# Causal attention in one transformer block: one score matmul and one row-maximum unit side by side, smaller PSUM buffers, the whole stage written out, an even plan of the maxima

## The reference

```python
def attn(x, W_Q, W_K, W_V, W_o):               # x: (1, 4096, 256), 16 heads of 16
    Q, K, V = (heads(W_Q), heads(W_K), heads(W_V))
    scores = jnp.einsum('bhqd,bhkd->bhqk', Q, K) / D_HEAD ** 0.5
    scores = scores + causal                   # -inf above the diagonal
    probs = jax.nn.softmax(scores, axis=-1)
    out = jnp.einsum('bhqk,bhkd->bhqd', probs, V)
    return out.transpose(0, 2, 1, 3).reshape(B, S, D_MODEL) @ W_o

x = L0_attn_x
xn = _layernorm(x, axis=-1)
x = x + attn(xn, ...) + moe(xn, ...)           # moe: 16 experts, each takes its 512 best tokens
```

## Time and profile before

| | us |
|---|---|
| median of three runs | 2787.35 (2768.93 to 2787.67) |
| the profiled execution | 2760.16 |
| its span, first to last instruction | 2758.4 |
| its attention blocks, 194.9 to 1947.7 | 1752.8 |

### The profile page before, as it was taken

One profiled execution on the slowest core, in us unless ns is written; L12 is line 12 of the kernel. 1 busy time (PEld: TensorE's weight loads), 2 busy tenths in 40 slices (PEclk: granted clock), 3 DMA queues, 4 the chain that ended last, 5 costly groups with the idle time before them and its releaser, 6 DMA issues. The chain is left out here.

```text
span 2758.4 us, 49577 instructions
## 1 busy us (share of the span) xinstructions
PE 2553.8 (93%) x16188; PEld 1434.8 (52%) x16190; DVE 1985.1 (72%) x3851; ACT 1432.8 (52%) x1899; POOL 237.6 (9%) x210
## 2 busy tenths in 40 slices
PE   7699999999999999999999999999799599999997
PEld 4454443334433334433333443333588488888886
DVE  6588788866888876788887788893455366666664
ACT  3205555665555565555666555568332244444543
POOL 0120000000000000000000000000110123333333
PEclk9859899998999998899999999999899799999999
DMA  7730000011000012000002100000121344444444
GB/s 254 271 110 25 9 9 9 1 57 52 11 9 9 9 38 58 22 11 9 9 9 59 44 9 3 3 3 3 56 68 53 124 115 123 123 123 123 123 123 123
DMA packets 141711, 165.12 MB, mean 60 GB/s; under 512 B 38848, under 2 KB 104896, under 8 KB 141504
## 3 DMA queue, kind: packets, MB, share of 16 engines
q1 hardware_dynamic: 128832, 144.08, 16.1%
q0 software_dynamic: 12672, 18.42, 3.9%
HBM read 115.50 MB, written 46.43 MB: 59 GB/s over the span
## 5 line engine op out<-in xcount | busy, mean ns | idle before, releaser
L794 DVE TENSOR_REDUCE a_mp<-a_pm 128x1 f32<-128x512 f32 (+3 forms) x2304 | 1332.1, 638 | 273.7 <-PE a_pm L873 169.7
L850 ACT ACTIVATE a_p<-a_ps 128x1024 f32<-128x1024 f32 (+3 forms) x1152 | 1039.9, 952 | 747.3 <-PE a_ps L914 513.5
L873 PE MATMUL a_pm<-a_k,a_q 48*128 48x512 f32 (+3 forms) x2304 | 874.6, 490 | 83.0 <-DVE a_mp L794 47.5
L873 PEld LDWEIGHTS a_pm<-a_k,a_q 48*128 48x128 f32 x2304 | 377.3, 195 | 757.6 <-DVE a_mp L794 689.1
L914 PE MATMUL a_ps<-a_q,a_k 50*128 50x512 f32 (+3 forms) x2304 | 662.4, 445 | 21.8 <-ACT a_p L850 13.1
L930 PE MATMUL a_po<-a_p,a_v 128*32 128x512 f32 (+3 forms) x4608 | 604.7, 599 | 0.1
L914 PEld LDWEIGHTS a_ps<-a_q,a_k 50*128 50x128 f32 x2304 | 288.2, 193 | 112.0 <-ACT a_p L850 83.6
L1321 DVE TENSOR_TENSOR e_hf<-e_g,e_pu 128x512 f32<-128x512 f32 x128 | 88.0, 688 | 175.0 <-ACT e_g L1278 164.3
L1354 PE MATMUL e_pg<-e_xt,e_wgup 128*128 128x512 f32 x768 | 198.9, 394 | 12.5 <-DVE e_xt L1304 12.5
L1278 ACT ACTIVATE e_g<-e_pg 128x512 f32<-128x512 f32 x128 | 76.6, 599 | 245.3 <-PE e_pu L1354 244.9
L1364 PE MATMUL e_po<-e_wdp,e_hp 128*128 128x256 f32 x1536 | 203.2, 284 | 0.0
(11 more groups left out here) (148 smaller groups left out, 1665.4 us busy)
## 6 DMA issues: line engine op xcount, KB each, us to landing
e_wgu<-in_wg SPq DMA_DIRECT2D x18, 1024.0 KB, 5.6
e_wgu<-in_wu SPq DMA_DIRECT2D x18, 1024.0 KB, 7.8
e_wd<-in_wd SPq DMA_DIRECT2D x18, 1024.0 KB, 10.1
qk_parts<-p_parts SPq DMA_DIRECT2D x32, 512.0 KB, 4.9
a_q<-qk_parts SPq DMA_DIRECT2D x192, 64.0 KB, 2.2
a_k<-qk_parts SPq DMA_DIRECT2D x192, 64.0 KB, 2.2
v_padded<-p_v SPq DMA_DIRECT2D x8, 1024.0 KB, 5.3
a_v<-v_padded SPq DMA_DIRECT2D x32, 256.0 KB, 2.9
```

Source lines behind the costliest of these rows:

```text
L794: eng.tensor_reduce(MP[j % 2][:, row, kc:kc + 1], ps[:, 0:w], AX.X, ALU.max).then_inc(s_mf, 1)
L850: eng.activation(PR[b % 2][:, 2 * a:2 * a + 2, off:GT], pS[a][:, :].rearrange("p (h n) -> p h n", h=2)[:, :, off:GT], ACT.Exp).then_inc(s_ ...
L873: last = eng.matmul(ps[:, 0:w], q, KT[tile, a, kc * GT:kc * GT + w], start=True, stop=kc < j)
```

## The change

In `attend`:

- The 32 tiles of the stage are one list `TILES`: groups 0 and 2 go up (`j` = 0 to 7), groups 1 and 3 go down (7 to 0). Nothing is looped; waits have constant values.
- `a_ps` is three single banks in place of two double ones, one head in each; `a_pm` has four banks in place of three. ScalarE takes 512 columns at a time, four activations for a block. A score waits for the exponential of the score three before it.
- `stream` orders TensorE's work of a block: a score, then a unit in the other row tile, a score, a unit, and so on; what is left over of either kind follows. The product of the block before comes last, then `max`, `out` and `bit`.
- `plan` deals out the units of all tiles over all 576 blocks at an even rate, each tile due four blocks before it starts and no more than seven tiles ahead (`SLOTS`). Only the 48 units of tiles 0 and 1 of the first group stay in `FIRST` (96 before).
- Two buffers of K and V (`a_k0`, `a_k1`); seven buffers for query tiles in place of five. The copy of the finished tile (`a_ot`) comes after the first four exponentials of the next tile.
- To make room, the transposed tokens go to DRAM in `project` and come back in `mix` (512 KB for each of eight groups), and the shared weights are copied from DRAM to DRAM in `project` and split in place in `attend`. The second pair of ScalarE copies in `project` is gone.

```diff
-        pM = [c.bank(f"a_pm{n}") for n in range(3)]
-        pS = [c.bank(f"a_ps{n}", n=2) for n in range(2)]
+        pM = [c.bank(f"a_pm{n}") for n in range(BANKS)]      # BANKS, HEADS, SLOTS = 4, 3, 7
+        pS = [c.bank(f"a_ps{n}") for n in range(HEADS)]
...
+            length = [400 + 3.4 * (GT - skipped(b)) for b in range(ALL)]
+            due = [START[t] - SPAN for t in range(LAST + 1)]
...
+                while rest and room >= cost(rest[0]) / 2:
+                    t = rest[0][1]
+                    if t >= SLOTS and b < START[t - SLOTS + 1] + 4:
+                        break
+                    room -= cost(rest[0])
+                    done += cost(rest[0])
+                    lists[b].append(rest.pop(0))
...
+        def stream():
+
+            out, tile = [], 0
+            for blk in range(ALL):
+                heads = [(a, i) for a in range(2) for i in range(2)]
+                units = [u for u in LISTS[blk] if u[0] == "unit"]
+                row = []
+                while heads or units:
+                    if heads:
+                        want = 1 - units[0][5] if units else 1 - tile
+                        h = next((h for h in heads if h[1] == want), heads[0])
+                        heads.remove(h)
+                        row.append(("score", *h))
+                        tile = h[1]
+                    if units:
+                        row.append(units.pop(0))
+                        tile = row[-1][5]
+                out.append(row)
+            return out
...
+                for n in range(NQ):
+                    if n < SLOTS:
+                        fetch_q(n)
+                    eng.wait_ge(s_one, 2 * n + 2)
+                    fetch_kv(0, n)
+                for t in range(LAST + 1):
+                    if ("max", t) not in IN:
+                        store_max(t)
...
+                for blk, (t, b) in enumerate(BLOCK):
+                    off = skipped(blk)
+                    if blk > 1:
+                        eng.wait_ge(s_pv, blk - 1)
+                    for n, (a, i) in enumerate(ORDER[blk], HG * blk):
+                        eng.wait_ge(s_st, n + 1)
+                        eng.activation(PR[blk % 2][:, 2 * a + i, off:GT], pS[n % HEADS][:, off:GT],
+                                       ACT.Exp).then_inc(s_ex, 1)
...
+                def score(blk, a, i):
+                    n = HG * blk + ORDER[blk].index((a, i))
+                    if n >= HEADS:
+                        eng.wait_ge(s_ex, n - HEADS + 1)
...
+                for blk, (t, b) in enumerate(BLOCK):
+                    for u in STREAM[blk]:
+                        if u[0] == "score":
+                            score(blk, *u[1:])
+                        else:
+                            use(u)
+                    if blk:
+                        product(blk - 1)
```

More of the change, by code:

```diff
@@ L635, in attend, with columns @@
[L635 to L642, removed]
+        SPAN = 4
+        BITS = 32
+        UNITS = [[("unit", t, a, r, kc, i) for kc in range(j + 1) for a in range(2) for r in range(NB) for i in range(2)]
+                 for t, (_, j) in enumerate(TILES)]
+        def columns(u):
+            _, t, a, r, kc, i = u
+            return GT if kc < TILES[t][1] else (r + 1) * P
@@ new lines, in plan @@
+            assert not rest
+            return first, lists
+        FIRST, LISTS = plan()
+        TAIL = [("out", LAST)]
+        USES = FIRST + [u for ls in LISTS for u in ls] + TAIL
+        AT = {u: n for n, u in enumerate(USES)}
+        IN = {u: b for b, ls in enumerate(LISTS) for u in ls}
+        def stream():
[16 more added lines that the diff above has]
+            return out
@@ L683, in attend @@
+        STREAM = stream()
+        ORDER = [[u[1:] for u in row if u[0] == "score"] for row in STREAM]
         qv = k.qkd.rearrange("w t (a i d) n -> w t i d a n", i=2, d=DH)
@@ new lines, in maxima, with bit, rows @@
+                def maxima(t, ps):
+                    eng.wait_ge(s_nm, t + 1)
+                    return eng.transpose(ps[0:HG * NB, 0:P], NM[t % 2][:, :], k.identf[:, :])
+                def bit(n, ps):
+                    eng.wait_ge(k.s_cn, n + 1)
+                    return eng.matmul(ps[:, 0:E], k.onesf[:, :], k.CN[:, :], start=True, stop=True)
+                def rows(t, ps):
+                    eng.wait_ge(s_ev, t + 1)
+                    for r in range(NB):
+                        last = eng.transpose(ps[:, r * P:(r + 1) * P], OT[t % 2][:, r * P:(r + 1) * P], k.identf[:, :])
+                    return last
@@ new lines, in product @@
+                def product(blk):
+                    t, b = BLOCK[blk]
+                    g, j = TILES[t]
+                    off = skipped(blk)
+                    eng.wait_ge(s_ex, HG * blk + HG)
+                    if b == 0 and t:
+                        eng.wait_ge(s_ev, t)
+                    for h in range(HG):
+                        last = eng.matmul(pO[h * VW:(h + 1) * VW, off:GT], V[g % 2][:, b, h * VW:(h + 1) * VW],
+                                          PR[blk % 2][:, h, off:GT], start=b == 0, stop=b == BLOCKS[t] - 1,
+                                          skip_group_check=True)
+                    last.then_inc(s_pv, 1)
@@ L961 @@
+                product(ALL - 1)
+                use(("out", LAST))
 HIGH, LOW = 0, 1
```

505 lines of the change are left out of this document (227 added, 278 removed).

## The result

The kernel after takes 2685.08 us (median of four runs, 2671.13 to 2716.87), the kernel before in the same comparison 2778.14 (2761.84 to 2787.67). The ratio is 0.9654, with a 95% interval of 0.9573 to 0.9736: 3.5% faster. The profiled execution took 2690.36 us, its span 2688.6.

A forecast was written before the change was run, and what follows sets the result against it. No engine was full; VectorE or ScalarE bound blocks by unit count. 2760.2 - 96 - 16 + 10 + 1 = 2659 us profiled, 27 us under the median, hence 2686 us; range 2585 to 2800.

The forecast's parts named there:

- the chain of banks: Attention blocks: score, exponential, fourth score, product through three score banks set 2.7 us a block for up to four units.
- The stage: Attention blocks, 1753 us before: full blocks -71, narrow -13, finished-tile copy -12, so 1657 us, a gain of 96.
- what is left: Attention stage: some 43 us for turned tiles, maxima, bits and lower-clock stretches, less 12 for the finished tile's copy.
- Pairing buys little: Attention blocks: running a score beside a unit gains little, because TensorE's array is not what a block waits for.
- The last rival: Attention blocks: score and unit don't run side by side, four units take 3.18 us, +159, 2845 us; chance 0.05.
- The rule that I weighed: Attention: packing row tiles speeds TensorE, not emptying of PSUM; VectorE's 1383 us stays, so five-unit blocks gain nothing from pairing.
- Start: Before the first exponential: only two tiles' maxima ahead, blocks begin at about 178.5 us; gain 16 us (8 to 20).
- Projection: Projection stage: 0.5 MB more DMA a group and 1.8 MB of shared weights cost +10 us (0 to 18).
- Mix and experts: `mix` waits at its start for a 512 KB load, +1 us (0 to 4); experts untouched.
- slower by the clock: Attention blocks with no or one unit get half clock, 4.1 us each; 90 such blocks reach 2815 us; chance 0.12.
- Only VectorE remains: Attention: chain overlaps between blocks, VectorE's 1383 us and 0.21 a block give stage 1504, total 2533 us; chance 0.10.
- What the plan gives, the order takes: Attention: scores behind units waiting for banks hold up ScalarE, 2.95 us for 341 blocks, +85, 2771 us; chance 0.18.

The follow-up runs named there:

- Run 6: Kernel after with the 32 routing bisection steps placed every 17 blocks, not every fourth of the last 140: 2754 us, ratio 0.985 to the kernel before.
- run 4: Kernel after with the plan placing units 1.3 times as fast as they fall due: 2868 us (2816 to 2922).
- the better order: Kernel after with the previous block's product ahead of the fourth score (run 3); with pairing undone on it, 2876 us, ratio 1.026 to the kernel before.
- run 1: Kernel after with pairing alone undone, units and scores of one row tile first, then those of the other: 3133 us (3074 to 3141).
- run 2: Kernel after with three banks for the units in place of four: 2853 us, ratio 1.023 to the kernel before.
- run 3: Kernel after with the previous block's product issued ahead of the fourth score: 2612 us, ratio 0.938 to the kernel before.
- 10: Kernel of run 3 with each score that has no unit beside it issued twice: 2663 us, ratio 0.957 to the kernel before.
- run 5: Kernel after with the product cut in two, two heads ahead of the third score, two behind the fourth: 2975 us, ratio 1.071 to the kernel before.
- 7: Kernel after with the edits of run 5 and Run 6 together: 2983 us, ratio 1.073 to the kernel before.

## Why the prediction was right, and where its steps were not

The forecast of 2686 us was met to 1 us. The direction and the chain of banks were right; that it is so close is luck, since wrong terms cancel. Against the profiled execution of before, the sum was -101 us; measured it is -70 (2760.16 to 2690.36). The profiled execution before happened to be a quick one, 27 us under the median known then; the shift back to the median that I added is 5 us the other way for the kernel after. With medians it is -93.

**The stage** was priced at -96 and brought -61. The prediction's own paces for the full and the narrow blocks add up to 1404 + 222 = 1626 us. The trace has 62 us more in the 48 blocks with half clock in them, 40 more in blocks with maxima, outs and bits and the ones close behind bits, and 37 less in ordinary blocks (four units 2.67 for 2.7; seven 3.7 for 4.2). The mis-sized term is "what is left", 43 less 12 us, which should have been 102. With bits, ScalarE's timeline of the last group shows it:

```profile
1431.10 2.31 ACT L861 ACTIVATE a_p<-a_ps 128x512 f32<-128x512 f32 x4 [0.61 <-PE a_ps L928]
1434.65 2.07 ACT L861 ACTIVATE a_p<-a_ps 128x512 f32<-128x512 f32 x4 [1.24 <-PE a_ps L928]
1437.32 2.07 ACT L861 ACTIVATE a_p<-a_ps 128x512 f32<-128x512 f32 x4 [0.60 <-PE a_ps L928]
1440.31 2.06 ACT L861 ACTIVATE a_p<-a_ps 128x512 f32<-128x512 f32 x4 [0.92 <-PE a_ps L928]
```

The block at 1437.32 has the bit. In the one at 1431.10, the second behind the bit before, the units start 0.60 us apart, at VectorE's pace: VectorE catches up what the bit took. Four blocks with one bit among them take 3.55 + 2.67 + 2.99 and 2.67, or 11.9 us, where four without take 10.7. In the last group half clock went from 34 us before to 86. The 86 are worth 37 us more than full clock would have taken, and the 34, at the same rate, an estimated 15; so some 22 of the 41 us that the group lost are the clock's.

The change moved the bits as well, which neither its description nor the prediction names. Before, each group had 8 of the 32; now all 32 stand in the last 140 blocks. Two of VectorE's lines in the last group, before and after (busy us, mean ns):

```profile
L437 DVE TENSOR_TENSOR r_ge<-scores,r_cand 128x512 bf16<-128x512 f32 x8 | 5.5, 692 | 0.3
...
L446 DVE TENSOR_TENSOR r_ge<-scores,r_cand 128x512 bf16<-128x512 f32 x32 | 22.1, 692 | 1.1
```

With its other operations a bit takes VectorE 2.1 us, so 24 more are an estimated 50 us of its work in this group. Run 6, with seven bits there, brings the group to 407.5 us, under the 416.7 of before, at 47 us of half clock: the loss of the last group goes with the bits' place, and so does most of the clock's fall there. For the stage as a whole, though, spreading them gained nothing.

**The chain of banks** was right: 2.67 for 2.7 us with four units and 2.65 with none (4). Five units took 2.9 to 3.0 for 3.0, which is VectorE's 0.60 a unit, as the prediction had it.

**"Pairing buys little"** was wrong. I reasoned that TensorE's array isn't what a block waits for. But the unit of the fourth score lies on that chain, between the score and the product; side by side it costs nothing, one behind the other 0.24 us. And without pairs the clock falls. Undone, it costs about 450 us here and about 260 on the better order: more than the whole gain. The last rival, with no overlap, had 159 us for it; the order alone cost 86 (1), and the clock, which the rival left out, 361. The rule that I weighed (the Trainium skill, TensorEngine Tiling (Array Packing), section PSUM Bottleneck) speaks of throughput; VectorE wasn't full here (395.9 of 444.3, 340.7 of 399.1 us in two groups), so in blocks of four units it didn't decide. By the same runs the fourth bank (run 2, about 170 us) and the even plan (run 4, over 130) are each worth more than the total. The parts don't add: with any one of the three undone, half clock is 1122, 359 or 456 us in place of 149, and that fall is charged to each of them in full.

**Start**: 16 us for 16 (15.5 without what projection gave). **Projection**: +10 forecast, -1 measured (the first DMA issue of the stage at 126.23, was 127.18). The DMA share was 1.04 with 384 GB/s, from 0.96 with 340: the load before was not what the queues could give, the end at nothing of my bound was the true one. **Mix and experts**: +1 forecast, +6.7 measured (806.6 to 813.3), half of it ahead of the first stored output, where the transposed tokens are loaded, and 2 us in one group whose granted clock was 0.93 in place of 1.00.

**The rivals.** The clock didn't leave 0.92 to 0.96 for the stage as a whole (0.96, the mean of the four windows by their lengths, at the upper end), so "slower by the clock" didn't come; its mechanism, at 37 us in the last group, did. "Only VectorE remains": no, it is busy 1403 of 1692 us. "What the plan gives, the order takes": a score held up behind a unit is rare (45 us of waits behind VectorE; the block of 3.55 us above is one), but run 3 shows that the order took 73 us all the same, by where it put the product. The stage, with 1692 us, missed the "near 1650" of the signs, and projection its 5 to 15 us; no tile's first block waited for its maxima.

**Open.** What makes the granted clock fall in one stretch and not in the next isn't settled. Few matmuls (10), bits (6) and empty blocks (4) move it about, none removes it. Only the kernels with the product in halves (5 and 7) are nearly free of it, with 9 and 23 us. Not run by themselves are the stage written out with constant waits, the 512-column activations and the two buffers of K and V; what each gives isn't known.

## What to carry to other kernels

Price a reordering on the chain from bank to bank, with every instruction that lies between the waiting one and the next long one: there a matmul that runs beside another is free, and one behind it cost 0.24 us here. Try each place for the longest absence of an engine among the work that it feeds: one place further up gave 73 us here, two places 37. When a change gathers small work in one stretch, price that stretch by itself. Give the clock a term of its own, from the rows at half clock before, and expect edits that each look small to move it by hundreds of microseconds.

## What the hardware showed that was not expected

TensorE was "busy" for 588.37 of 596.80 us in the last group of run 1 and was granted 0.61; in the kernel after it was busy for 358.96 of 391.10 in group 2 and had 1.00. Part of that is circular, since a matmul at half clock is busy for longer. But within run 1 groups 1 and 2 were busy for 98% and 99% and had 0.99 and 0.76. The busy share of the profile doesn't foretell the clock. The Trainium skill, TensorE: Matmul & The Clock Gate, section What's actually happening, says that the gate follows how busy the engine was; these rows show that the profile's busy time is not that measure. The same matmuls had half clock for 1122 us one row tile after the other and for 149 us in pairs, and the kernel with two half products a block (run 5), whose matmuls use all 128 rows, for 9.

Four matmuls of two heads in two column tiles take 1.05 us and eight of four heads in four 1.07: a product of this width has one price, whether two or four of its column tiles are filled.
